# The rank-one updates of a feed-forward layer: summed into the weights ahead of the matmuls, or kept as matmuls of their own

## The chip, the cores and the metric

The kernel runs on one core of one Trainium2 chip. The metric is the device time of one launch in microseconds; of several runs the median is given. Engines are named as in the profile: PE (TensorE, matmuls), DVE (VectorE), ACT (ScalarE), POOL (GpSimd) and SP (SyncE, which issues all transfers here).

## What is computed

Two layers on 16 tokens. A "token" here is one batch entry, a matrix of 256 rows and 256 columns; `ctx` has the same shape.

```python
x = x + xattn0(ctx, layernorm(x))          # latent attention, 8 heads
x = x + ffn0(layernorm(x))                 # W1: 1024x256, W2: 256x1024
x = x + xattn1(layernorm(x), ctx, ctx)     # one head, 256 wide
x = x + ffn1(layernorm(x))                 # 8 experts, gate/up/down, routed

def ffn0(x):
    lt = x[:, 1:17, :]                     # 16 rows of each token
    even, odd = lt[:, ::2, :], lt[:, 1::2, :]
    m1 = (even[:, :4, :, None] * odd[:, :4, None, :]).reshape(Bx, Hx, Dx)
    m2 = (even[:, 4:, :, None] * odd[:, 4:, None, :]).reshape(Bx, Dx, Hx)
    h = x @ W1.T + scale * einsum('bsd,bhd->bsh', x, m1) + b1
    out = gelu(h) @ W2.T + scale * einsum('bsh,boh->bso', gelu(h), m2) + b2
```

So each token has weights of its own: W1 plus `scale` times four outer products of normalised rows of the token, one for each quarter of the 1024 hidden rows, and W2 plus four more.

## The kernel before

The kernel has two halves. The first, `latent_attention`, does the first attention for one token after the other: turns b = 0 to 15, of which 1 to 14 are a loop. The second, `ffn_attention_experts`, does the rest. Its turn t holds two things side by side: the chain of token t (feed-forward layer, second attention, routing weights) and the eight experts of token t-1. Turn 1 stands by itself, because it also splits the weights of experts 2 to 7; turns 2 to 14 are a loop, turn 15 is the last with a chain and turn 16 has experts only. The chain of token 0, which has no turn of experts to stand in, is put beside the last turn of the first half (b = 15).

All products are of float32 values split into a high and a low half in the type fp32r: a "high" copy on ACT, the difference "low" on DVE, and three matmuls for each product (high by high, high by low, low by high; lines 1818 to 1820).

The order of the work of each engine is written out by hand: each engine has its own function `turn`, which lists its instructions in the order in which its queue runs them, and semaphores say what each waits for. Between two experts stands one link of the chain: an expert has its `gate` and `up` products (24 matmuls), then ACT's silu, DVE's `hidden` (gate by up, line 1464), ACT's high copy and DVE's `hidden_low` (line 1468), then its `down` product (12 matmuls) and DVE's `weigh` (line 1481), which adds the weighted result to the token's sum `acc`. The banks of `gate` and `up` are single: `up` of the next expert waits for `hidden` of the one before. The end of a turn on PE is `gate` and `up` of expert 7, `down` 6, `transposed(t, "C")`, `z_fill(t + 1)`, `down` 7, the routing product, then `gate` and `up` of expert 0 of token t.

The chain's links are, in order: A, the transposed and normalised token (`transposed`, line 1829); H, four products into the hidden layer (`h_fill`); the gelus; Y, two products out of it (`y_fill`); the second residual; B (normalised and transposed again); V, Q, S, T, O, the parts of the second attention; C, the third normalised and transposed matrix; and R, the routing. In each of A, B and C the mean and variance are taken on DVE, the inverse deviation on POOL (`rstd_of`, lines 1031 and 1033) and the normalised matrix on DVE (`norm_apply`, line 1420).

The rank-one updates are done with matmuls. `odd_rows` (POOL) spreads the odd rows; `z_fill` multiplies them into the token (four matmuls, line 1836); `z_high` and `z_low` scale and split that; `h_fill` adds a matmul of 256 columns (line 1846) to each of its eight groups. For W2, the odd rows lie as 16 extra columns between the pieces of W2 (`W2ROW` = 272 columns), so that `y_fill` gives their products as well; `g_high` and `g_low` split these, `g_fill` transposes them (line 1858), `gt_copy` copies them and `y_update` adds them into Y (line 1864). The even rows are split by `even_high` and `even_low`, and SP brings them into place with 24 small transfers for each token, `updates_of`, into `b_up`; `h_fill` waits for these (`up_in`). W1 and W2 are loaded and split once, at the start.

Other lines in the rows below: L326 is the first half's scaling of the attention weights (`normalise_probs`, POOL), L333 its bias sum; L1044 is `bias_x2` on POOL; L1458 is `context_low`, the low half of the context on DVE; L1493 is `copy_low`, which takes the low half of a transposed matrix out of PSUM.

Of the kernel before, what the change touches and what calls it, by code (L numbers as in the profile page):

```python
# [12 lines left out]
P = 128  # L13
B = 16
# [56 lines left out]
class Beside:  # L71


    early: Callable
    beside: Callable
# [43 lines left out]
def latent_attention(nc, ctx, mem, x, ctx_in, x1, g_media, b_media, g_lat, b_lat, Wq, bq, Wkv, bkv, Wo, bo):  # L119
# [112 lines left out]
    def sections_of(eng, body):  # L232

        body(sections["first"], 0, False, True)
        with eng.Fori(1, B - 1) as b:
            body(Order(loop_names, loop_first - F, sections["first"], F, b), b, True, True)
        body(last, B - 1, True, False)

# [17 lines left out]
    def sync(sp, other):  # L256
# [24 lines left out]
        def turn(order, b, prev, nxt):  # L281
# [13 lines left out]
            if not prev:  # L295
                other.early(0)
        sections_of(sp, turn)
# [5 lines left out]
    def gpsimd(pool, other):  # L303
# [38 lines left out]
        def turn(order, b, prev, nxt):  # L342
            for h in range(H):
# [12 lines left out]
                if not prev:  # L356
                    other.early(h)
        sections_of(pool, turn)

    def scalar(act, other):  # L360
# [60 lines left out]
        def turn(order, b, prev, nxt):  # L421
            i = 0
            for h in range(H):
# [18 lines left out]
                if not prev:  # L442
                    other.early(h)
                i += n
# [5 lines left out]
    def vector(dve, other):  # L450
# [115 lines left out]
        def turn(order, b, prev, nxt):  # L566
            i = 0
            for h in range(H):
# [34 lines left out]
                if not prev:  # L603
                    other.early(h)
                i += n
# [145 lines left out]
def ffn_attention_experts(nc, ctx, mem, first, x1, ctxT, out, W1T, b1, W2T, b2, scale, Wq, bq, Wk, bk, WvT, bv, Wg, Wu,  # L751
# [21 lines left out]
    BANK = {("H", 0): 0, ("H", 1): 1, ("H", 2): 2, ("H", 3): 3, "Y0": 0, "Y1": 1, "G": 2, "V": 2, "B": 0,  # L773
            "Q": 1, "S": 3, "T": 0, "A": 2, "O": 1, "C": 3, "Z": 2, "R": 0}
# [6 lines left out]
    def put(region, name, shape, dt=F32, raw=False, odd=None):  # L781
# [4 lines left out]
    up1, up2 = put("low", "up1", [P, NL, D], F32R, odd=1), put("low", "up2", [P, D], F32R, odd=1)  # L786
    w2h, (w2_raw, w2l) = put("low", "w2h", [P, W2ROW * HC + 16], F32R, odd=1), put(
        "low", "w2l", [P, W2ROW * HC + 16], F32R, raw=True, odd=1)
    od = put("low", "od", [P, DC, P], F32R, odd=1)
    zm_part, zm = put("low", "zm_part", [P, S], F32R), put("low", "zm", [P, S], F32R, odd=0)  # L790
    gr = put("low", "gr", [P, ST, P], F32R)
    ROWS = 32
    ev1 = put("low", "ev1", [ROWS, 2, D], F32R)
    ev2 = put("low", "ev2", [ROWS, 2, NL, A4], F32R)
# [4 lines left out]
    factors = put("low", "factors", [P, 4])  # L799
    lscale, lmask, tinv, thalf = (factors[:, n:n + 1] for n in range(4))  # L800
# [31 lines left out]
    gt = put("values0", "gt", [P, ST, P], F32R, odd=1)  # L832
# [18 lines left out]
    OWN = {("H", 0): ps_c, ("H", 1): ps_x, ("H", 2): ps_c, ("H", 3): ps_x, "Y0": ps_c, "Y1": ps_x, "A": ps_c, "Z": ps_c,  # L851
# [1373 lines left out]
```

## Time and profile before

| | us |
|---|---|
| median of 3 runs | 1987.82 |
| lowest and highest | 1985.39, 1988.81 |
| the profiled execution | 1991.09 |
| its span in the trace | 1989.3 |
| mean granted TensorE clock | 0.995 of 2.4 GHz |

The profile is of one execution of its own. Its span runs from the first instruction to the last; the execution's time has 1.8 us more around it. Turn b of the first half is read between two of its residual sums, a turn of the second half as the stretch after which the pattern of instructions repeats. In the trace names that start with `a_` belong to the first half and those with `b_` to the second. Starts and durations are in us; a matmul's duration overlaps the next one's, so that what a matmul costs is read from the start of one to the start of the next.

### The profile page before, as it was taken

The page shows a single profiled execution, that of the slowest core. Times are in us where ns is not written, and L with a number is a line of the kernel's source. Part 1 is how long each engine was busy: PE and PEld are TensorE (multiplying, and loading weights), DVE is VectorE, ACT ScalarE, POOL GpSimd, SP SyncE. Part 2 cuts the span into 40 slices and gives each one's busy share as a digit, 9 for nine tenths or more (in the row PEclk, how much of TensorE's full clock was granted, in tenths as well). Part 3 has the DMA queues.
Part 4 walks back from the last instruction along what each step waited for, and adds up shares of the span by engine and source line. Part 5 has one row for each costly group of instructions (what it writes and reads, how often), then busy time and mean ns, then how long its engine had stood idle before and what let it go on. Part 6 is the DMA issues. An engine that isn't in the chain of part 4 may idle for free.

```text
span 1989.3 us, 41475 instructions
## 1 busy us (share of the span) xinstructions
PE 1927.2 (97%) x14078; PEld 1803.2 (91%) x14078; DVE 1367.9 (69%) x3408; ACT 1115.5 (56%) x2334; POOL 407.1 (20%) x650
## 2 busy tenths in 40 slices
PE   7999999999999999999987899999999999999998
PEld 6788888888888888888886899999999999999998
DVE  7877776776777776776746566766666666766665
ACT  5655565555655565555655655554555555544553
POOL 2222222222222222222213511111111101111100
PEclk9999999999999999999999999999999999999999
DMA  4000000000000000000012200000000000000000
GB/s 162 12 22 21 11 11 21 21 21 5 16 21 21 11 11 21 21 21 6 10 34 89 67 15 15 12 17 17 11 16 16 17 12 17 12 17 12 17 7 12
DMA packets 47211, 44.51 MB, mean 22 GB/s; under 512 B 6848, under 2 KB 45376, under 8 KB 47168
## 3 DMA queue, kind: packets, MB, share of 16 engines
q1 hardware_dynamic: 47168, 43.96, 6.9%
q8 instruction: 25, 0.41, 0.1%
q14 instruction: 18, 0.15, 0.0%
HBM read 34.77 MB, written 8.39 MB: 22 GB/s over the span
## 4 chain that ended last, share of the span: by engine, by line
PE 83%; DVE 7%; ACT 5%; issue 3%; POOL 1%; SPq 1%; DMA 0%; DVEq 0%; ACTq 0%; POOLq 0%
PE ring L618 9%; PE ring L620 9%; PE ring L619 9%; PE ring L1820 7%; PE ring L1818 7%; PE ring L1819 7%; PE ring L671 4%; PE sim L1818 3%; PE sim L1819 3%; PE sim L1820 3%; PE sim L618 3%; PE sim L620 2%; PE sim L619 2%; PE ps_x L1818 2%; PE ps_x L1820 2%
## 5 line engine op out<-in xcount | busy, mean ns | idle before, releaser
L411 ACT ACTIVATE a_pr<-sim,a_nmax 128x512 f32<-128x512 f32 x256 | 174.5, 689 | 208.4 <-DVE a_nmax L537 208.3
L1818 PE MATMUL ring<-b_xch,b_weh 128*128 128x256 f32 x1024 | 289.5, 283 | 1.7 <-DVE b_act_e L1464 1.7
L1819 PE MATMUL ring<-b_xcl,b_weh 128*128 128x256 f32 x1024 | 285.7, 279 | 0.0
L1820 PE MATMUL ring<-b_xch,b_wel 128*128 128x256 f32 x1024 | 285.6, 279 | 0.0
L326 POOL TENSOR_SCALAR a_pr<-a_pr,a_rinv 128x512 f32<-128x512 f32 x256 | 183.1, 729 | 498.3 <-DVE a_rinv L547 495.4
L1818 PEld LDWEIGHTS ring<-b_xch,b_weh 128*128 128x128 f32 x1024 | 192.3, 188 | 1.9 <-DVE b_act_e L1464 1.9
L1819 PEld LDWEIGHTS ring<-b_xcl,b_weh 128*128 128x128 f32 x1024 | 193.0, 188 | 0.0
L1820 PEld LDWEIGHTS ring<-b_xch,b_wel 128*128 128x128 f32 x1024 | 192.1, 188 | 0.0
L1464 DVE TENSOR_TENSOR b_act_e<-b_act_e,ring 128x512 f32<-128x512 f32 x128 | 87.9, 687 | 116.7 <-PE ring L1820 102.4
L528 DVE TENSOR_TENSOR a_ptl<-ring,a_pth 128x512 fp32r<-128x512 f32 x256 | 163.9, 682 | 3.1 <-ACT a_pth L401 2.0
L515 DVE SCALAR_TENSOR_TENSOR a_ktl<-ring,a_bkv_s,a_kth 128x512 fp32r<-128x512 f32 x128 | 95.3, 744 | 102.1 <-ACT a_kth L391 102.1
L537 DVE TENSOR_REDUCE a_nmax<-sim 128x1 f32<-128x512 f32 x256 | 163.8, 681 | 1.6 <-PE sim L620 1.6
L1179 ACT ACTIVATE b_heh<-b_act_e 128x512 fp32r<-128x512 f32 x128 | 81.1, 633 | 132.1 <-DVE b_act_e L1464 132.0
L618 PE MATMUL ring<-a_pth,a_vh 128*128 128x256 f32 x512 | 142.8, 279 | 3.7 <-DVE a_ptl L528 3.7
L524 DVE TENSOR_TENSOR a_vl<-ring,a_vh 128x512 fp32r<-128x512 f32 x128 | 88.4, 691 | 81.7 <-ACT a_vh L399 81.5
L620 PE MATMUL ring<-a_pth,a_vl 128*128 128x256 f32 x512 | 142.6, 279 | 0.0
L619 PE MATMUL ring<-a_ptl,a_vh 128*128 128x256 f32 x512 | 142.5, 278 | 0.0
L401 ACT ACTIVATE a_pth<-ring 128x512 fp32r<-128x512 f32 x256 | 140.2, 607 | 3.6 <-PE ring L671 3.6
L399 ACT ACTIVATE a_vh<-ring 128x512 fp32r<-128x512 f32 x128 | 76.8, 600 | 109.8 <-PE ring L620 109.8
L1175 ACT ACTIVATE b_act_e<-ring 128x512 f32<-128x512 f32 x128 | 76.4, 597 | 104.3 <-PE ring L1820 103.7
L671 PE MATMUL ring<-ident,a_pr 128*128 128x128 f32 x1024 | 133.3, 272 | 1.5 <-DVE a_ktl L515 1.2
L671 PEld LDWEIGHTS ring<-ident,a_pr 128*128 128x128 f32 x1024 | 118.2, 140 | 14.8 <-DVE a_ktl L515 1.5
(378 smaller groups left out, 6246.0 us busy)
## 6 DMA issues: line engine op xcount, KB each, us to landing
a_c_in<-in_ctx_in SPq DMA_DIRECT2D x16, 256.0 KB, 2.6
a_x_in<-in_x SPq DMA_DIRECT2D x16, 256.0 KB, 2.9
a_x_res<-in_x SPq DMA_DIRECT2D x16, 256.0 KB, 2.6
x_between<-a_x_out SPq DMA_DIRECT2D x16, 256.0 KB, 2.2
b_x_s<-x_between SPq DMA_DIRECT2D x16, 256.0 KB, 2.6
b_up<-b_ev SPq DMA_DIRECT2D x256, 1.0 KB
out_x<-b_acc SPq DMA_DIRECT2D x16, 256.0 KB, 2.2
b_ct_raw<-in_ctxT SPq DMA_DIRECT2D x15, 256.0 KB, 2.6
```

What stands on the lines that cost most here:

```text
L326: nc.gpsimd.tensor_scalar(pr[:, h % 2, t, :], pr[:, h % 2, t, :], rinv[:, h % 2, t:t + 1], 1.0, ALU.mult, ALU.mult).then_inc(prob_ready, 1)
L401: nc.scalar.activation(pth[:, :, name[2] * P:(name[2] + 1) * P], bank[:].rearrange("p (k q) -> p k q", k=KT), ACT.Copy).then_inc(ring_hi, 1)
L411: nc.scalar.activation(pr[:, h % 2, t, :], sim[t][:], ACT.Exp, bias=nmax[:, h % 2, t:t + 1], accum_out=rsum[:, h % 2, t:t + 1]).then_inc(e ...
L528: nc.vector.tensor_tensor(ptl[:, :, cols], bank[:].rearrange("p (k q) -> p k q", k=KT), f32(pth[:, :, cols]), ALU.subtract).then_inc(ring_ ...
L537: nc.vector.tensor_reduce(nmax[:, h % 2, t:t + 1], sim[t][:], AX.X, ALU.max, negate=True)\
L618: nc.tensor.matmul(out, lh, rh, start=(n == 0), stop=False)
L619: nc.tensor.matmul(out, lh, rl, start=False, stop=False)
L620: last = nc.tensor.matmul(out, ll, rh, start=False, stop=(n == len(parts) - 1))
L671: last = nc.tensor.transpose(bank[:, k * P:(k + 1) * P], pr[:, h % 2, t, k * P:(k + 1) * P], ident[:])
L1818: nc.tensor.matmul(out, lh, rh, start=(n == 0), stop=False)
L1819: nc.tensor.matmul(out, lh, rl, start=False, stop=False)
L1820: last = nc.tensor.matmul(out, ll, rh, start=False, stop=(n == len(parts) - 1 and not more))
```

## The change

The rank-one updates are summed into W1 and W2 themselves, for each token, one turn ahead of its chain. All rank-one matmuls and what feeds them (`odd_rows`, `z_fill`, `z_high`, `z_low`, `g_high`, `g_low`, `g_fill`, `gt_copy`, `y_update`, `even_high`, `even_low`, `updates_of`) go, and `W2ROW` is 256.

In their place, for token n: SP loads the first 32 rows of the token (`rows_load`); DVE, POOL and DVE normalise them (`rows_stats`, `rows_rstd`, `rows_apply`); SP writes 16 of them out and reads them back, the even ones spread over all partitions (`even_b`, 1 MB of SBUF) and the odd ones transposed (`rows_spread`); POOL scales the odd ones (`odd_scaled`) and makes eight updates, four pieces of W1 and four of W2, each of two products and a sum (`update`). The pieces are split anew for each token: the high halves on ACT (`weight_high`), the low halves of W1 on POOL and those of W2 on DVE (`weight_low`). W1 and W2 are loaded again for each token (1 MB each), W1 after the last of the H products and W2 after the Y products of the token before. `h_fill` waits for all low halves of W1, `y_fill` for those of W2.

```diff
+        def update(n, w, q):
+            a, b = divmod(q, 2)
...
+            for k in range(2):
...
+                nc.gpsimd.tensor_scalar(part, row, by, 1.0, ALU.mult, ALU.mult).then_inc(update_made, 1)
+            take(w_in[w], n * 16 + 16)
+            pool.wait_ge(update_made, 2 * number + 2)
+            nc.gpsimd.tensor_tensor(piece, piece, added, ALU.add).then_inc(w_eff[w], 1)
+
+        def weight_low(n, w, q):
+            take(w_hi[w], n * 4 + q + 1)
+            raw, high, low = (w_piece(w, q, tile) for tile in W[w])
+            nc.gpsimd.tensor_tensor(low, raw, f32(high), ALU.subtract).then_inc(w_lo[w], 1)
```

POOL's turn, of which only the three `rstd_of`, `row_shifts`, the two biases and `odd_rows` stood there before:

```diff
-            def turn(t, chain, more, warm):
+            def turn(t, chain, more, more2, warm):
...
+                if more:
+                    odd_scaled(t + 1)
+                    if not warm:
+                        update(t + 1, "1", 0)
                 if chain:
                     rstd_of(t, "B")
                     row_shifts(t)
                     bias_x2(t)
...
+                    update(t + 1, "1", 1)
                     rstd_of(t + 1, "A")
+                    update(t + 1, "1", 2)
+                    update(t + 1, "1", 3)
                     bias_x1(t + 1)
+                    update(t + 1, "2", 0)
+                    if more2:
+                        rows_rstd(t + 2)
+                    update(t + 1, "2", 1)
...
                 if chain:
                     rstd_of(t, "C")
                 if more:
...
+                        update(t + 1, "2", 2)
+                    update(t + 1, "2", 3)
+                    if not warm:
+                        for q in range(4):
+                            weight_low(t + 1, "1", q)
```

The chain's links on PE move by about half a slot: V goes ahead of `down` 2 and B behind it, Q ahead of `down` 3, S between `gate` and `up` of expert 5, T behind `down` 4, O and the next token's A ahead of `down` 5, C ahead of `down` 6. ACT's and DVE's orders follow. The end of DVE's turn:

```diff
                 if chain:
                     copy_low(t, "C", xcl[:], xch[:])
+                if more2:
+                    rows_apply(t + 2)
+                weigh(i, 6)
                 if more:
-                    z_low(t + 1)
-                weigh(i, 6)
+                    weight_low(t + 1, "2", 0)
+                    weight_low(t + 1, "2", 1)
                 weigh(i, 7)
+                if more:
+                    weight_low(t + 1, "2", 2)
+                    if not warm:
+                        weight_low(t + 1, "2", 3)
                 if chain:
                     hidden(t, 0)
```

In turn 1, twelve subtractions of expert weights (experts 4 to 7) move from POOL to DVE, and on ACT the high halves of the second group of experts move behind the gelus.

The first half's turn b = 14 is taken out of its loop, and what token 0 needs ahead of its chain is put there (`ahead`): its rows, POOL's updates of W1 and ACT's high halves, and the first of W2. Turn b = 15 (`beside`) holds the rest for token 0, and the updates for token 1. In the second half, turn 14 is taken out of the loop as well, since token 15 is the last to have updates made.

## Rows read from the trace of the kernel before

**Rows 1.** The page, its first part: busy us of each engine, share, instructions.

```profile
PE 1927.2 (97%) x14078; PEld 1803.2 (91%) x14078; DVE 1367.9 (69%) x3408; ACT 1115.5 (56%) x2334; POOL 407.1 (20%) x650
```

**Rows 2.** Turn windows: us, busy PE PEld DVE ACT POOL (instructions), PEclk, DMA.

```profile
940.94:1004.87 63.93, 63.57 (x402) 56.24 (x401) 44.91 (x97) 36.44 (x82) 15.35 (x26) 1.00 0.04 13
1004.87:1093.94 89.07, 71.43 (x509) 65.90 (x507) 51.74 (x114) 49.75 (x107) 19.78 (x31) 0.96 0.21 67
1102.60:1169.20 66.60, 59.58 (x468) 58.83 (x467) 40.91 (x109) 39.38 (x75) 31.43 (x33) 0.92 0.06 18
1281.40:1337.60 56.20, 55.57 (x473) 55.20 (x472) 37.70 (x109) 30.90 (x60) 8.36 (x15) 1.00 0.05 15
```

**Rows 3.** Timeline of PE: start, us, line, operation; matmuls into H, into Y.

```profile
1283.52 0.28 PE L1846 MATMUL sim<-b_zm,b_up 128*128 128x256 f32 x1
...
1283.99 0.28 PE L1818 MATMUL sim<-b_xth,b_w1h 128*128 128x256 f32 x1
...
1291.96 0.29 PE L1818 MATMUL sim<-b_w2h,b_hh 128*128 128x272 f32 x1
...
1292.95 0.29 PE L1820 MATMUL sim<-b_w2h,b_hl 128*128 128x272 f32 x1
```

**Rows 4.** Timeline of PE: transposes of B and C, up of expert 1.

```profile
1306.61 0.28 PE L1820 MATMUL ps_c<-b_wvh,b_ctl 128*128 128x256 f32 x1
1307.42 0.52 PE L1829 MATMUL sim<-ident,b_ln 128*128 128x128 f32 x3 [0.54 <-DVE b_ln L1420]
...
1328.23 0.28 PE L1820 MATMUL ring<-b_weh,b_hel 128*128 128x256 f32 x1
1328.61 0.66 PE L1829 MATMUL ring<-ident,b_ln 128*128 128x128 f32 x4
...
1335.87 0.28 PE L1818 MATMUL ring<-b_xch,b_weh 128*128 128x256 f32 x1
```

**Rows 5.** Timeline of DVE at the end of the same turn.

```profile
1329.99 0.69 DVE L1493 TENSOR_TENSOR b_xcl<-ring,b_xch 128x512 fp32r<-128x512 f32 x1 [0.70 <-ACT b_xch L1198]
...
1331.89 0.88 DVE L1481 SCALAR_TENSOR_TENSOR b_acc<-ps_x,b_wts,b_acc 128x256 f32<-128x256 f32 x2
1334.50 0.69 DVE L1464 TENSOR_TENSOR b_act_e<-b_act_e,ring 128x512 f32<-128x512 f32 x1 [1.73 <-PE ring L1820]
```

**Rows 6.** Forms by line: count, ns min/median/max, first and last start.

```profile
L1458 DVE TENSOR_TENSOR b_ctl<-b_ct_raw,b_cth x15: 680/685/686, 1117.1 to 1910.1; 128x512 fp32r<-128x512 f32 x15
L1458 DVE TENSOR_TENSOR b_ctl<-b_gel,b_cth x1: 1410/1410/1410, 1057.4 to 1057.4; 128x512 fp32r<-128x512 f32 x1
...
L326 POOL TENSOR_SCALAR a_pr<-a_pr,a_rinv x256: 692/699/1135, 30.2 to 1077.4; 128x512 f32<-128x512 f32 x128
...
L1044 POOL TENSOR_TENSOR b_x_s<-b_x_s,b_bv_b x16: 1286/1309/1732, 1058.2 to 1925.9; 128x512 f32<-128x512 f32 x16
...
L1031 POOL TENSOR_SCALAR b_rows<-b_mv x48: 192/194/433, 990.7 to 1943.8; 128x2 f32<-128x2 f32 x48
```

**Rows 7.** Timeline of POOL and DVE in the first half's last turn.

```profile
1047.57 1.71 POOL L333 TENSOR_TENSOR a_x_res<-a_x_res,a_bo_b 128x512 f32<-128x512 f32 x1
...
1048.07 1.76 DVE L1432 TENSOR_TENSOR b_wvl<-b_wvl_raw,b_wvh 128x512 fp32r<-128x512 f32 x1
```

**Rows 8.** Timeline of PE: the matmuls behind two long waits.

```profile
1014.71 0.55 PE L1818 MATMUL ps_c<-b_xth,b_w1h 128*128 128x256 f32 x1 [5.58 <-DMA b_up<-b_ev]
...
1115.94 0.56 PE L1818 MATMUL sim<-b_w2h,b_hh 128*128 128x272 f32 x1 [3.25 <-DVE b_hl L1488]
```

**Rows 9.** Windows behind these two waits, columns as in rows 2.

```profile
1013.00:1019.00 6.00, 4.29 (x20) 4.32 (x21) 0.00 (x0) 0.90 (x3) 0.03 (x1) 0.50 0.28 89
1115.00:1121.00 6.00, 5.06 (x22) 5.09 (x23) 3.47 (x7) 4.45 (x9) 1.54 (x3) 0.50 0.14 45
```

**Rows 10.** DMA issues: count, KB each, us from issue to landing.

```profile
b_w2l_raw<-in_W2T SPq DMA_DIRECT2D x1, 1024.0 KB, 8.1
```

More of the change, by code:

```diff
@@ L1020, in rest @@
             sp.wait_ge(out_done, 16 * B + 16)
-        return Beside(early, beside, rest)
+        return Beside(early, ahead, beside, rest)
     def gpsimd(pool):
@@ L1309, in beside @@
                 copy_high(1, "A", xth[:])
+            if (h, done) == (7, ("O", 6)):
+                for q in range(4):
+                    weight_high(1, "1", q)
             if (h, done) == (7, ("T", 7, 1)):
@@ L1323, in rest, with turn, experts @@
         def rest():
-            def turn(t, chain, more, warm):
+            def turn(t, chain, more, more2, warm):
                 i = t - 1
-                for e in warm_in(0) if warm else ():
-                    for j in range(3):
-                        expert_high(e, j)
+                def experts(slot):
+                    for e in warm_in(slot) if warm else ():
+                        for j in range(3):
+                            expert_high(e, j)
+                experts(0)
                 silu(i, 1)
@@ L1396, in turn @@
                     hidden_high(t, 0)
+                if more and warm:
+                    weight_high(t + 1, "2", 3)
+                if chain:
                     tanh_high(t)
             sections_of(act, turn)
-        return Beside(early, beside, rest)
+        return Beside(early, ahead, beside, rest)
     def vector(dve):
@@ L1724, in beside, with turn @@
                 distances(0)
+                for q in range(4):
+                    weight_low(1, "2", q)
         def rest():
-            def turn(t, chain, more, warm):
+            def turn(t, chain, more, more2, warm):
                 i = t - 1
@@ L1809, in turn, with product @@
                     distances(t)
+                if more and warm:
+                    weight_low(t + 1, "2", 3)
             sections_of(dve, turn)
-        return Beside(early, beside, rest)
+        return Beside(early, ahead, beside, rest)
     def tensor(pe):
-        def product(out, parts, left_h, left_l, right_h, right_l, more=False):
+        def product(out, parts, left_h, left_l, right_h, right_l):
             for n, part in enumerate(parts):
@@ L1819, in product @@
                 nc.tensor.matmul(out, lh, rl, start=False, stop=False)
-                last = nc.tensor.matmul(out, ll, rh, start=False, stop=(n == len(parts) - 1 and not more))
+                last = nc.tensor.matmul(out, ll, rh, start=False, stop=(n == len(parts) - 1))
             return last
@@ L1830, in transposed @@
             last.then_inc(full[name], 1)
-        def z_fill(n):
-            pe.wait_ge(od_ready, n + 1)
-            for c in range(DC):
-                for k, x in enumerate((xth, xtl)):
-                    last = nc.tensor.matmul(bank(n, "Z")[:, 0:S], od[:, c, :], x[:, c, :],
-                                            start=(c == 0 and k == 0), stop=(c == DC - 1 and k == 1))
-            last.then_inc(full["Z"], 1)
         def h_fill(t, n):
```

556 lines of the change are left out of this document (292 added, 264 removed).

## Prediction

> **What bounds the kernel now.** I read the busy times of the page first: TensorE (PE) is busy in 97% of the span and no other engine in more than 69% [rows 1]. So time is gained only by taking PE work away or by closing one of the short gaps in which PE waits. Next I read the windows, one per turn [rows 2]: a steady turn of the second half takes 56.2 us and PE is busy in 55.57 of it, while GpSimd (POOL) works 8.36 us and VectorE (DVE) 37.7. The first turn, which also splits the weights of six experts, takes 66.6 us; the last turn of the first half, with the chain of token 0 beside it, takes 89.07 with PE busy in 71.4. These two have the long gaps [rows 8] and stretches at half the clock [rows 9], and the rest is near solid. Then I read the PE timeline for the step from one matmul to the next and for the gaps at the chain's links [rows 3, 4], the end of a turn on DVE [rows 5], and what a DVE and a POOL instruction do to each other [rows 6, 7].
>
> **What leaves PE in a steady turn.** A 256-column matmul is issued every 0.1175 us (1283.52 to 1283.99 is four), a 272-column one every 0.124 (1291.96 to 1292.95 is eight) [rows 3]. Gone are eight rank-one matmuls of `h_fill`, four of `z_fill`, two transposes of `g_fill` and two matmuls of `y_update`: 16 x 0.1175 = 1.88 us (the two transposes are narrower, so this is a few hundredths too much). The 48 matmuls of `y_fill` become 256 columns wide: 48 x 0.0065 = 0.31. Moving the links by half a slot gives each longer between its parts: the wait ahead of the transposes of B (1306.61 to 1307.42, less one step, 0.69) and the one ahead of those of C (1328.23 to 1328.61, less one step, 0.26) [rows 4] should close. Sum 3.14: a turn of 53.1 if nothing new stalls.
>
> **What is added.** On POOL an update is two products of 128x256 and one sum of 128x512. A tensor_scalar takes 0.70 us at 512 columns and 0.19 at 2 [rows 6], so about 0.44 at 256; a sum takes 1.31. One update is 2.2 us, eight are 17.5; four subtractions for the low half of W1 add 5.2, the row statistics and the scaling of the odd rows about 1.5. With the 8.36 of before, less about 1.4 of copies, POOL works some 31 us of 56: it has the room, but not at any moment. ScalarE (ACT) gets eight copies (about 5 us) onto 30.9 and loses its small copies: covered. DVE gets four subtractions for W2 (0.685 each, 2.7 us) and loses 1.5 or so: covered by its 18 us of idle time, if they can be spread. SyncE (SP) loses 24 small transfers per token and gets two reloads of 1 MB; W2's took 8.1 us from issue to landing [rows 10] and now has half a turn, so I cost it at nothing; if it were late by half a turn, the first sum into W2 would stand still on POOL with all behind it. The spreading of the rows waits on SP for POOL's last sum into W2 of the turn before, and the store of a finished token stands behind it there; nothing reads that store within the turn.
>
> **The collision.** DVE and POOL hold each other up. The subtraction L1458 (two operands in SBUF) took 0.68 to 0.69 us fifteen times and 1.41 once [rows 6], the time at which POOL ran; POOL's L1044 rose from 1.31 to 1.73, L326 from 0.70 to 1.13, L1031 from 0.19 to 0.43. In the first half a DVE subtraction of 1.76 us that began under a POOL sum of 1.71 ended 0.55 after it [rows 7]. Reading from PSUM it isn't so held: L1493 takes its 0.69 us as always [rows 5]. Today POOL works so little that this hardly shows. After the change it works all the time, and DVE has nine two-SBUF subtractions of its own in a turn and four new ones.
>
> The Trainium skill (page "SBUF — State Buffer", section "SBUF: two separate sides") states the port pair that VectorE and GpSimd share as an exclusive lock which the first comer holds for its whole instruction. The 1.41 of [rows 6] is less than a subtraction behind a whole POOL sum would be, the 0.55 after the end in [rows 7] is what such a lock gives. By the page alone each of four subtractions would wait out a whole sum, and the stall worked out next would be about 4.0 us in place of 2.25.
>
> **Where the collision lies on the path.** At the end of a turn DVE does the low half of C, two weighings, and then `hidden(t, 0)`, which frees the bank that PE's `up` of expert 1 writes next. Before: the low half of C ends at 1329.99 + 0.69 = 1330.68, `hidden` starts at 1334.50 (it waits for PE) and ends at 1335.19, PE's `up` starts at 1335.87 [rows 4, 5]: 3.82 us between, 0.68 to spare. After: the transposes of C go ahead of down 6, twelve matmuls earlier (+1.41), and `z_fill` is gone (-0.47), so 4.76 us between, 5.44 with the slack. In it DVE must now do the rows (0.3), two weighings of 0.87 and four subtractions for W2: 0.3 + 1.75 + 4 x 0.685 = 4.8, which fits. But POOL does its own four subtractions for W1, 1.31 us each, at that very time (both sets are put last in the turn). At 1.41 each the four take 5.64 and the sum is 7.7: PE waits 2.25 us, where before it waited for nothing. If they don't meet it is 0; if each waits out a whole POOL sum (1.31 + 0.55 = 1.86 each, 7.4 together), 4.0. I take 2.25, by the row of the same DVE instruction.
>
> **Smaller new waits.** `y_fill` starts 0.94 us sooner after the matmuls that feed the gelus; the inverse deviations of B and C (0.19 + 0.70 us on POOL) can stand behind an update of 2.2 us each; DVE's subtractions of the hidden values, at 1.41 when they meet POOL, hold the `down` products; `s_fill` and `o_fill` have other neighbours. None of these is in the trace of before. Each lies between 0 and the 2.2 of one update; I take 0.3 to 0.6 each, 1.7 together (bounds 0 and 3).
>
> So a steady turn is 53.1 + 2.25 + 1.7 = 57.0, +0.8 (bounds -1.9 without the end stall and with half of the small ones, +3 with the longest end stall), 13 turns: +10.4.
>
> **The other turns.** In the first half's last turn PE waits 5.58 us for the small transfers into `b_up`, [rows 8] and runs at half clock (0.50, 1.2 GHz) for the 6 us behind that wait [rows 9]: both go, 5.58 + 3.0, and 2.2 of PE work, 10.8 in all. Against it stands POOL, which gets updates for tokens 0 and 1 between its normalisations, DVE held by them, and the deviation of C behind updates; I take 3 back (bounds 0 and 8): -8. In the turn before, 63.9 us and PE busy in 63.6 [rows 2], all added work is cost: seven updates and three subtractions, 19 us, onto POOL's 15.4, in front of normalisations that PE's transposes wait for, and DVE waits for the loaded rows: +4 (bounds 0 and 8). The first turn of the second half: ACT splits fewer expert weights ahead of the gelus, so the 3.25 us wait of `y_fill` [rows 8] and the half-clock stretch behind it [rows 9] (6 us, 3.0) can go, and PE work of 2.2; DVE takes twelve subtractions over (8.3 us) with POOL beside it: I take 5.4 back, -3 (bounds 0 and -7). The turn of the last chain has no updates: -2. Sum 10.4 - 8 + 4 - 3 - 2 = +1.4 on the profiled 1991.1 us (its span is 1989.3), 1992.5. The median of the runs shown lies 3.3 below the profiled one: 1989.
>
> **Rivals.** *The collision misses PE (chance 0.27).* DVE's four subtractions wait for ACT's copies, which follow POOL's sums one by one; if they fall between POOL's own subtractions, or POOL is done before, the end stall is gone and a turn is about 54.3: 13 x -1.9 = -24.7, with -8, +2, -4 and -2 for the other turns: -37, 1951. For it: DVE is idle a third of the turn. Against it: the orders put both at the end. *The stall takes the clock along (0.10), slower.* In the trace PE's waits of 3.25 and 5.58 us [rows 8] were each followed by some 6 us at 1.2 GHz [rows 9]; in the steady turn, whose gaps are under 1 us, the clock is full (1.00 of 2.4 GHz) [rows 2]. From an end stall of about that length on, each turn would lose 3.0 us on top, and win back the small waits (1.5), which a slow PE doesn't meet: 57.0 + 1.3 + 3.0 - 1.5 = 59.8, 13 x 3.6 = +47, about 2035. By the whole-instruction lock of the page above (4.0) this is what would happen; the row of 1.41 speaks against it. *POOL is the bound (0.03).* If its 31 us, stretched by DVE, came to more than the turn leaves ahead of `h_fill`, the turn would follow POOL; 45 us even with each sum at 1.73, so no: some 2010. *It is all hidden (0.02)*: PE work gone is made up by waits for the same DVE work, 1988.
>
> **How the numbers follow.** Forecast 0.58, 1989 us, its own range 1976 to 2004. The range for 8 in 10 takes in half of the faster rival and the upper bounds of the end stall without the clock: 1951 to 2014. About 0.2% (4 us) is what a measurement of this kernel can tell from no change. Of the forecast's 0.58 I put 0.14 below 1984, 0.20 within and 0.24 above 1992: faster 0.14 + 0.27 = 0.41, same 0.22, slower 0.24 + 0.13 = 0.37.
>
> **What would show it.** In the changed kernel's windows a steady turn with PE busy in 53 us and 57 long; in its PE timeline a gap of about 2 us at the first matmul of `up` of expert 1, released by DVE's `hidden`; L1458's kin, the W2 subtractions, at 1.4 us and not 0.69; no `b_up` gap and no 0.50 stretch in the 89 us turn. I am wrong if the W2 subtractions take 0.69, if they are done ahead of the low half of C, or if a gap above 3 us stands elsewhere in each turn.

## The result, and the profile of the changed kernel

| | before | after |
|---|---|---|
| median, us | 1986.76 | 2030.41 |
| lowest, highest | 1985.39, 1988.81 | 2029.02, 2031.3 |
| profiled execution, its span | 1991.09, 1989.3 | 2029.02, 2027.2 |

(The kernel before has one run more here than in the table ahead of the prediction.) The ratio is 1.0215, 95% interval 1.0199 to 1.0231: the change costs 2.1%, and the time lies above the predicted range. The page's first part of the changed kernel (after), to be held against [rows 1]:

```profile
PE 1913.3 (94%) x13822; PEld 1778.5 (88%) x13822; DVE 1492.3 (74%) x3442; ACT 1139.7 (56%) x2362; POOL 836.2 (41%) x1036
```

PE lost 256 matmuls and 14 us of busy time, yet the span grew by 37.9. POOL's work doubled, as meant, and DVE is busy 124 us longer. The windows of the four kinds of turn, with the columns of [rows 2] and in the same order (the last two turns of the first half, the first of the second, a steady one):

```profile
934.59:999.61 65.02, 62.93 (x395) 55.03 (x395) 46.92 (x102) 39.23 (x87) 41.42 (x53) 1.00 0.15 43
999.61:1084.38 84.77, 70.95 (x489) 65.72 (x487) 54.96 (x112) 51.62 (x108) 51.58 (x60) 0.94 0.34 101
1093.10:1168.30 75.20, 60.67 (x454) 59.18 (x453) 60.42 (x126) 40.59 (x77) 47.37 (x46) 0.89 0.24 69
1282.20:1341.40 59.20, 54.71 (x457) 53.45 (x455) 45.48 (x111) 32.60 (x61) 35.96 (x41) 1.00 0.23 68
```

Each stretch measured between the same two events of both traces, in the second half from the `hidden` of expert 0 at the end of one turn to that of the next (the predicted column is the prediction's own step; the window of b = 14 in [rows 2] starts 1.2 us ahead of its residual sum, so that the stretch of before is 62.7 and not 63.9):

| stretch | predicted, us | measured, us |
|---|---|---|
| first half, b = 0 to 13 | 0 | -7.6 |
| b = 14 | +4 | +2.3 |
| b = 15 | -8 | -4.3 |
| t = 1 | -3 | +8.3 |
| t = 2 to 14 (13 turns) | +10.4 | +39.4 |
| t = 15 and 16 | -2 | -0.3 |
| sum | +1.4 | +37.8 (spans: 37.9) |

Two lines carry the miss: the steady turns, 29.0 us beyond the forecast, and the first turn of the second half, 11.3 us. The steady turns' waits on PE's timeline (start, duration, and in brackets the idle time and its releaser; the wait runs from the start of the matmul before, less one step of 0.1175):

```profile
1282.21 0.28 PE L1917 MATMUL ring<-b_xch,b_wel 128*128 128x256 f32 x1
1284.23 0.38 PE L1915 MATMUL ring<-b_xch,b_weh 128*128 128x256 f32 x1 [1.74 <-DVE b_act_e L1564]
...
1296.55 0.36 PE L1915 MATMUL sim<-b_w2h,b_hh 128*128 128x256 f32 x1 [0.83 <-DVE b_hl L1588]
...
1322.04 0.33 PE L1990 MATMUL sim<-ident,b_pr 128*128 128x128 f32 x1 [0.78 <-ACT b_pr L1322]
...
1332.60 0.33 PE L1926 MATMUL ring<-ident,b_ln 128*128 128x128 f32 x1 [0.57 <-DVE b_ln L1507]
...
1335.07 0.39 PE L1915 MATMUL ps_x<-b_weh,b_heh 128*128 128x256 f32 x1 [0.40 <-DVE b_hel L1568]
```

The first is the end stall: 1284.23 - 1282.21 - 0.12 = 1.90 us at `up` of expert 1, released by DVE's `hidden`. Counted from the matmul ahead of each in the same way, the others are 0.99 at Y, 0.93 at T, 0.73 at C and 0.56 at `down` 7; with 0.32 at O the six make 5.43. 59.20 less these is 53.8, in which the matmuls just behind a wait take longer (0.33 to 0.39 us for 0.28).

DVE and POOL in the same turn, DVE first, in two fences. "x2" is two instructions with their time together:

```profile
1331.32 1.22 DVE L1507 TENSOR_SCALAR b_ln<-b_x_s,b_mv,b_rows 128x256 f32<-128x256 f32 x2
...
1333.83 1.18 DVE L1568 TENSOR_TENSOR b_hel<-b_act_e,b_heh 128x512 fp32r<-128x512 f32 x1 [0.70 <-ACT b_heh L1288]
...
1336.64 2.70 DVE L1525 TENSOR_TENSOR b_w2l<-b_w2l_raw,b_w2h 128x512 fp32r<-128x512 f32 x2
...
1340.04 2.69 DVE L1525 TENSOR_TENSOR b_w2l<-b_w2l_raw,b_w2h 128x512 fp32r<-128x512 f32 x2
```

```profile
1296.72 1.30 POOL L1120 TENSOR_TENSOR b_w1l_raw<-b_w1l_raw,b_rank_one 128x512 f32<-128x512 f32 x1 [9.69 <-DMA b_w1l_raw<-in_W1T]
...
1304.64 0.19 POOL L1064 TENSOR_SCALAR b_rows<-b_mv 128x2 f32<-128x2 f32 x1 [6.62 <-DVE b_mv L1500]
...
1330.95 1.44 POOL L1117 TENSOR_SCALAR b_rank_one<-b_even_b,b_odd 128x256 f32<-128x256 f32 x2
...
1337.05 6.82 POOL L1125 TENSOR_TENSOR b_w1l<-b_w1l_raw,b_w1h 128x512 fp32r<-128x512 f32 x4
```

The four W2 subtractions at the turn's end take 1.35 us each (2.70 / 2), beside POOL's four W1 subtractions of 1.71 each (6.82 / 4): the meeting that the prediction expected. But two other DVE operations, on the chain's path, are stretched as well: the two halves of the normalisation of C to 0.61 each, beside products of POOL, and `hidden_low` of expert 7 to 1.18. And POOL stands idle for 9.69 us in front of its first sum of the turn, waiting for the reload of W1, and for 6.62 more behind it, waiting for DVE's variance of B. In its order one update of eight stands ahead of B; the last two and the four W1 subtractions come at the end.

### The profile page after: what moved, and what is told of

It is laid out like the page before. It is cut to its first block, busy times and chain, and to the rows that moved or that the text cites. A ratio compares the mean times of both kernels' runs of the same rounds, so it can differ in the third digit from the quotient of the medians.

```text
span 2027.2 us, 41696 instructions
## 1 busy us (share of the span) xinstructions
PE 1913.3 (94%) x13822; PEld 1778.5 (88%) x13822; DVE 1492.3 (74%) x3442; ACT 1139.7 (56%) x2362; POOL 836.2 (41%) x1036
## 4 chain that ended last, share of the span: by engine, by line
PE 59%; DVE 19%; ACT 11%; issue 9%; POOL 1%; DVEq 1%; DMA 0%; ACTq 0%; POOLq 0%; SPq 0%
PE ring L632 9%; PE ring L634 9%; PE ring L633 9%; PE ring L685 4%; DVE b_acc L1581 3%; PE sim L632 3%; PE ring L1915 2%; PE ring L1917 2%; PE sim L634 2%; PE ring L1916 2%; PE sim L633 2%; PE sim L1915 2%; DVE b_act_e L1564 2%; PE sim L1917 2%; PE sim L1916 2%
## 5 line engine op out<-in xcount | busy, mean ns | idle before, releaser
L1117 POOL TENSOR_SCALAR b_rank_one<-b_even_b,b_odd 128x256 f32<-128x256 f32 x256 | 174.4, 694 | 10.5 <-POOL b_odd L1094 4.9
L1284 ACT ACTIVATE b_act_e<-ring 128x512 f32<-128x512 f32 x128 | 76.2, 595 | 163.7 <-PE ring L1917 163.2
L1568 DVE TENSOR_TENSOR b_hel<-b_act_e,b_heh 128x512 fp32r<-128x512 f32 x128 | 118.2, 923 | 60.0 <-ACT b_heh L1288 59.7
L1120 POOL TENSOR_TENSOR b_w1l_raw<-b_w1l_raw,b_rank_one 128x512 f32<-128x512 f32 x64 | 83.7, 1308 | 129.7 <-DMA b_w1l_raw<-in_W1T 125.5
```

Of the source, the lines that this page charges most:

```text
L1117: nc.gpsimd.tensor_scalar(part, row, by, 1.0, ALU.mult, ALU.mult).then_inc(update_made, 1)
```

## Experiments

A time without an interval is of one run, beside one run of the kernel before on the same chip.

**Links alone.** Does the new order of the links cost something by itself, or only the added work? No token but the first gets rows, updates, reloads or new splits; all use the weights of token 0.

```diff
         def update(n, w, q):
+            if not (isinstance(n, int) and n == 0):
+                return
...
-                    pe.wait_ge(w_lo["1"], t * 4 + 4)
+                    pe.wait_ge(w_lo["1"], 4)
```

> The changed kernel without its added work: from token 1 on no rows are loaded, no updates made, W1 and W2 neither loaded again nor split again (every token uses the weights of token 0). The new order of the links and the missing matmuls stay. If the added work makes the stalls (collision of DVE and POOL, or work that comes late), a steady turn falls from 59.15 us to 53.1 to 53.8 and the whole to about 1945. If the new order of the links makes them, gaps of about 1 us stay ahead of the Y products, the T products and the transposes of C, and a turn takes 56 or more, the whole 1985 or more.

Measured: 1953.1 us, before beside it 1985.92. A steady turn (columns as in [rows 2]), a little above the range of the first expectation and far below the second; and PE's matmul at its longest wait:

```profile
1495.60:1550.00 54.40, 53.90 (x455) 53.23 (x455) 36.82 (x103) 28.68 (x53) 6.73 (x9) 1.00 0.05 15
```

```profile
1545.79 0.36 PE L1934 MATMUL sim<-b_w2h,b_hh 128*128 128x256 f32 x1 [0.30 <-DVE b_hl L1607]
```

Three waits are left, counted as above: Y 0.46, C 0.25 and `down` 7 0.27, together 0.98. So 54.40 - 0.98 = 53.4 is the turn's PE work, 0.3 above the 53.1 of the prediction, and the new order costs 1.0 us of waits by itself. The other 4.8 (59.20 - 54.40) come with the added work. They don't come from PE, which does the same in both.

**Without products and sums.** The 24 operations of the updates become eight fills of one column; reloads, high halves and all eight subtractions stay where they are.

```diff
-                nc.gpsimd.tensor_scalar(part, row, by, 1.0, ALU.mult, ALU.mult).then_inc(update_made, 1)
...
-            nc.gpsimd.tensor_tensor(piece, piece, added, ALU.add).then_inc(w_eff[w], 1)
+            nc.gpsimd.memset(rank_one[:, q % 2, 0:1], 0.0).then_inc(w_eff[w], 1)
```

> The changed kernel without the products and sums of the updates: in the place of each update POOL writes one column. Reloads, high halves, the four W1 subtractions on POOL and the four W2 subtractions on DVE stay. If DVE is held by whatever POOL does, most of POOL's 24 us per turn are gone, only the subtractions can meet: the gaps ahead of T, C and down 6 fall from 1.05, 0.85 and 0.68 to below 0.4, and a turn to 54 to 55.5. If the gaps come from the order of the queues and the added instructions of DVE and ACT, they stay and a turn takes 58 or more.

Measured: 1994.88 us, a steady turn 57.2; neither expectation was met. The W2 subtractions are short, and the end stall is gone, since POOL now does its W1 subtractions earlier. But there they meet the normalisation of C and `hidden_low` of expert 7. The form by its line, then DVE, POOL and PE in one steady turn (line numbers are this kernel's):

```profile
L1516 DVE TENSOR_TENSOR b_w2l<-b_w2l_raw,b_w2h x60: 668/672/1784, 1090.6 to 1899.9; 128x512 fp32r<-128x512 f32 x60
```

```profile
1547.90 2.26 DVE L1498 TENSOR_SCALAR b_ln<-b_x_s,b_mv,b_rows 128x256 f32<-128x256 f32 x2
...
1551.46 1.64 DVE L1559 TENSOR_TENSOR b_hel<-b_act_e,b_heh 128x512 fp32r<-128x512 f32 x1 [0.70 <-ACT b_heh L1279]
```

```profile
1547.45 5.10 POOL L1116 TENSOR_TENSOR b_w1l<-b_w1l_raw,b_w1h 128x512 fp32r<-128x512 f32 x4
...
1550.22 0.65 PE L1917 MATMUL ring<-ident,b_ln 128*128 128x128 f32 x4 [1.62 <-DVE b_ln L1498]
```

The normalisation took 1.13 a half, `hidden_low` 1.64 and not 0.69, and PE waits for both: 1.78 at C and 1.03 at `down` 7, counted as above. Products and sums aren't needed for this: POOL's subtractions do it by themselves where they fall on the chain.

**POOL's time without its reads.** Is DVE held by POOL's reads, or by any work of POOL? Here the updates and the W1 subtractions become chains of small fills, which read nothing (36 fills for the four subtractions, 2.98 us in place of the 5.10 above). They are shorter than what they replace: POOL is busy in 19.0 us of a turn, not in 36.0.

```diff
+            for k in range(7):
+                nc.gpsimd.memset(tile[:, k * 256 // 7:(k + 1) * 256 // 7], 0.0)
             take(w_in[w], n * 16 + 16)
...
+            for k in range(11):
+                last = nc.gpsimd.memset(tile[:, 256 + k * 256 // 11:256 + (k + 1) * 256 // 11], 0.0)
+            last.then_inc(w_eff[w], 1)
```

> The changed kernel with POOL as busy as before but reading nothing in its added work: each product, sum and subtraction is replaced by small fills of about the same time in all (the weights keep no update and no low half of W1). If POOL's reading is what holds DVE, the W2 subtractions on DVE fall from 1.35 and more to 0.69, the end stall from 2.0 to below 0.6, and a turn to 53.5 to 55. If only the lateness of POOL's queue counts, or fills hold DVE as well, a turn stays at 58 to 59.2.

Measured: 2050.32 us, a steady turn 61.4: slower than the change itself, and neither expectation was met. A subtraction beside fills (DVE, then POOL), the form of the normalisation (ns min/median/max), then DVE, POOL and PE at one C, and PE's windows from the wait on:

```profile
1495.99 0.69 DVE L1568 TENSOR_TENSOR b_hel<-b_act_e,b_heh 128x512 fp32r<-128x512 f32 x1 [0.70 <-ACT b_heh L1288]
...
1495.91 0.65 POOL L1115 MEMSET b_rank_one<- 128x23 f32 x11
1496.49 0.51 POOL L1112 MEMSET b_rank_one<- 128x36 f32 x7
```

```profile
L1507 DVE TENSOR_SCALAR b_ln<-b_x_s,b_mv,b_rows x96: 394/409/4656, 989.3 to 2001.4; 128x256 f32<-128x256 f32 x96
```

```profile
1512.17 4.97 DVE L1507 TENSOR_SCALAR b_ln<-b_x_s,b_mv,b_rows 128x256 f32<-128x256 f32 x2
...
1513.70 2.98 POOL L1124 MEMSET b_w1l<- 128x56 f32 x36
...
1517.20 0.69 PE L1926 MATMUL ring<-ident,b_ln 128*128 128x128 f32 x2 [4.32 <-DVE b_ln L1507]
```

```profile
1512.60:1517.20 4.60, 0.28 (x4) 0.07 (x2) 4.60 (x3) 0.00 (x0) 4.08 (x57) 0.89 0.00 0
1517.20:1521.00 3.80, 3.80 (x18) 3.80 (x19) 2.32 (x5) 3.19 (x6) 0.00 (x0) 0.50 0.00 0
```

A subtraction of two operands in SBUF isn't held by fills: the low half of a hidden matrix takes its 0.69 with fills beside it from start to end. (The W2 subtractions are short as well, and the end stall is gone, but POOL is idle by then, so that these show nothing of fills.) But one half of the normalisation, with a single operand in SBUF and 0.41 us long, took 4.65, until the whole row of fills was through. PE then waits 4.32 us, and runs at 0.50 (1.2 GHz) behind it, every turn. So the two kinds of DVE operation are held by different work of POOL: the subtraction only by work that reads, the normalisation, which the prediction left out, by either.

**The first turn of the second half.** In it DVE's four W2 subtractions for token 1 stand ahead of what the gelus wait for (DVE, then POOL, of after):

```profile
1092.06 5.79 DVE L1525 TENSOR_TENSOR b_w2l<-b_w2l_raw,b_w2h 128x512 fp32r<-128x512 f32 x4
...
1092.59 4.71 POOL L1132 TENSOR_TENSOR b_wel<-b_wel_raw,b_weh 128x512 fp32r<-128x512 f32 x3 [8.92 <-ACT b_weh L1275]
...
1108.10 0.55 PE L1915 MATMUL sim<-b_w2h,b_hh 128*128 128x256 f32 x1 [5.92 <-DVE b_hl L1588]
```

Moving them behind the gelus on DVE was to take the wait away.

```diff
                 distances(0)
-                for q in range(4):
-                    weight_low(1, "2", q)
...
                         gelu_low(t, n)
+                    if warm:
+                        weight_low(t, "2", n)
```

> The changed kernel with the four W2 subtractions of token 1 moved on DVE from ahead of the first hidden product of the second half's first turn to behind each of its four gelus. If these (5.8 us beside POOL's subtractions of expert weights) delay the gelus and so the Y products, the gap of 6.2 us there falls below 3 and the first turn from 75.2 us to 68 to 71. If ACT's order or POOL delays the gelus, the gap stays above 5.

Measured: 2029.57 us, the turn 76.2 where it was 75.5 (counted as in the table of stretches). The same wait is now released by the moved subtractions themselves:

```profile
1110.16 0.55 PE L1915 MATMUL sim<-b_w2h,b_hh 128*128 128x256 f32 x1 [7.04 <-DVE b_w2l L1525]
```

So the expectation missed. Y needs all four, and both places lie ahead of it: the move leaves them on its path. A later experiment takes them off DVE.

**POOL held back for the normalisation.** If held normalisations are the cause, POOL should wait, after the inverse deviations of A and C, until DVE has normalised.

```diff
                     rstd_of(t + 1, "A")
+                    pool.wait_ge(ln_ready["A"], t + 2)
...
                     rstd_of(t, "C")
+                    pool.wait_ge(ln_ready["C"], t + 1)
```

> The changed kernel with two waits more on POOL: behind the inverse deviations of A and C it stands still until DVE has normalised. All work stays. If it is POOL's work that stretches the normalisation (0.73 us for two alone, 1.22 in the steady turn, 4.97 under a row of fills), both take 0.73 to 0.8 and the gap ahead of the transposes of C falls from 0.85 to about 0.4, the one ahead of T from 1.05 to 0.6; POOL's work ends later by what it waited (about 4 us), so that the end stall grows from 2.0. If DVE's normalisation is long for another reason, it stays at 1.2.

Measured: 2070.85 us, before beside it 1988.14. The normalisations are free in the steady turns (0.73 for two), so it was POOL's work that stretched them. But the gap ahead of C didn't fall, it grew, and all is much slower (the form by line, then DVE and PE at one C, and POOL's first product behind the A that follows):

```profile
L1509 DVE TENSOR_SCALAR b_ln<-b_x_s,b_mv,b_rows x96: 394/411/1347, 989.6 to 2023.5; 128x256 f32<-128x256 f32 x96
```

```profile
1281.51 0.73 DVE L1509 TENSOR_SCALAR b_ln<-b_x_s,b_mv,b_rows 128x256 f32<-128x256 f32 x2 [3.24 <-POOL b_rows L1066]
...
1282.30 1.12 PE L1928 MATMUL ring<-ident,b_ln 128*128 128x128 f32 x4 [3.76 <-DVE b_ln L1509]
...
1329.29 0.98 POOL L1117 TENSOR_SCALAR b_rank_one<-b_even_b,b_odd 128x256 f32<-128x256 f32 x2 [5.41 <-DVE b_ln L1509]
```

POOL stands 5.41 us for the normalisation of A, its updates come later, and the inverse deviation of C stands behind them: DVE waits 3.24 us for it. The turn shown, of 1280 to 1342, ran at a granted clock of 0.94, which is a part of the price. Freeing the operation by holding up POOL moves the wait into POOL's own queue.

**POOL's order, all work kept.** POOL makes one update ahead of B, idle for 9.69 and 6.62 us around its sum, and has two updates and all W1 subtractions at the end. Here it makes the first products while W1 is loading, does three W1 sums ahead of B, puts each W1 subtraction between two W2 updates, and waits for the normalised C before its last piece. ACT's high halves move forward with it, and one W2 subtraction on DVE.

```diff
+                    odd_scaled(n)
+                    products(n, "1", 0)
+                    products(n, "1", 1)
+                    added_in(n, "1", 0)
...
+                    update(n, "2", 0)
+                    weight_low(n, "1", 0)
...
+                    rstd_of(t, "C")
+                    take(ln_ready["C"], t + 1)
+                if more:
+                    update(n, "2", 3)
+                    weight_low(n, "1", 3)
```

> The changed kernel with POOL's work spread over the steady turn: both first products while W1 is on its way, three sums into W1 ahead of the deviation of B, the W1 subtractions between the sums into W2, POOL still while C is normalised; ACT's high copies and one of DVE's W2 subtractions moved to fit. Every instruction is kept. If the stall at the end comes from both subtractions being put there together, it falls from 2.0 to below 0.7 and a turn from 59.15 to 55.5 to 57, the whole to 1975 to 2000. If the collisions cost the same wherever they stand, a turn stays above 58.

With it, in a second kernel, the W2 subtractions for token 1 are done by POOL ahead of the first turn:

```diff
-                for q in range(4):
-                    weight_low(1, "1", q)
+                for w in "12":
+                    for q in range(4):
+                        weight_low(1, w, q)
```

> As the run before, and the four W2 subtractions of token 1 made by POOL ahead of the second half's first turn instead of by DVE at its start. If DVE's 5.8 us there delay the gelus, the gap of 6.2 us ahead of the Y products falls below 2.5 and the first turn from 75.2 us to 69 to 72, the whole by 3 to 6. If POOL is late with them, the gap stays above 5 and is released by them.

Measured: 2004.36 and 1995.16 us, before 1988.14 beside both. The steady turn is 57.15 and its end stall 0.32 instead of 1.9: the stall fell as the first branch said, the turn and the whole ended just above its ranges. In the second kernel the first turn of the second half is 68.9 instead of 75.5 (76.5 in the first kernel), and its wait at Y:

```profile
1104.90 0.36 PE L1970 MATMUL sim<-b_w2h,b_hh 128*128 128x256 f32 x1 [1.61 <-DVE b_hl L1642]
```

That is 9.2 us less in all, more than the 3 to 6 expected: 7.5 are this turn, and 1.8 are the last one, where a stretch at half clock is missing. So the same instructions, in another order and four of them on another engine, take 35 us less than after.

**The waits that were left** (C, `down` 7, Y, T) in three further steps, each on top of the one before. First: `down` 1 ahead of Y, the maxima ahead of the normalisation of A, that of C ahead of the weighing, the deviation of C earlier on POOL.

```diff
+                down(i, 1)
                 if chain:
...
                         y_fill(t, k)
-                down(i, 1)
```

> As the run before (POOL's work spread, token 1's W2 subtractions on POOL), and each of the gaps left in its steady turn of 57.2 us given cover: down of expert 1 ahead of the Y products instead of behind them; DVE takes the softmax maxima ahead of A's normalisation, and C's normalisation ahead of a weighing; POOL takes C's deviation ahead of a W1 subtraction. If the gaps (1.1 ahead of Y, 0.66 ahead of T, 0.42 ahead of O, 1.35 ahead of the transposes of C) are single late links, they fall to 0.3 and less, a turn to 54.3 to 55.3 and the whole to 1955 to 1975, below the kernel before. If DVE as a whole is too late because POOL holds it (6 us more of it in a turn), closing one gap opens the next and a turn stays at 56.3 or more, the whole above 1982.

Measured: 1992.15 against 1990.47, ratio 1.0008 (0.9998 to 1.0018). The turn is 56.5: Y and T are closed, but C waits 1.35 and `down` 7 1.37 (the 1.47 of the next expectation counts the step in). That is the second branch: closing the gaps opened others, where the next piece of POOL's work met the next DVE operation. Second: the deviation of C ahead of the third W2 sum, a weighing behind `hidden_low` 7, no W2 subtraction ahead of it.

```diff
-                    update(n, "2", 2)
+                    products(n, "2", 2)
...
+                    added_in(n, "2", 2)
                     weight_low(n, "1", 2)
```

> As the run before, with the two gaps of 1.47 us that were left in its steady turn taken on: POOL takes C's deviation ahead of the third sum into W2, DVE the weighing of expert 5 behind the hidden product of expert 7 and its first W2 subtraction behind the low half of C; in the second half's first turn ACT takes the tanh of the routing ahead of the last W2 copy. If these gaps stem from where single instructions stand, both fall below 0.4, a turn to 53.7 to 55 and the whole to 1955 to 1972. If POOL's hold on DVE only moves on, the same time shows at the first matmul of up of expert 1 or at down 7 and a turn stays at 56 or more, the whole above 1982.

Measured: 1980.19 against 1990.05, ratio 0.9952 (0.9935 to 0.9968), the turn 55.6, between the two branches. C is closed. One long wait is left, in ten of the eleven turns from 3 to 13 at `down` 7 (DVE, POOL, PE of one of them):

```profile
1603.34 1.83 DVE L1622 TENSOR_TENSOR b_hel<-b_act_e,b_heh 128x512 fp32r<-128x512 f32 x1
...
1603.33 1.29 POOL L1133 TENSOR_TENSOR b_w1l<-b_w1l_raw,b_w1h 128x512 fp32r<-128x512 f32 x1
...
1605.22 0.39 PE L1966 MATMUL ps_x<-b_weh,b_heh 128*128 128x256 f32 x1 [1.37 <-DVE b_hel L1622]
```

A POOL subtraction that starts 0.01 us before `hidden_low` makes that 1.83 us, 1.14 more than its 0.69, and PE waits 1.37. Third: POOL waits for `hidden_low` of expert 7 before its last W1 subtractions, and the last piece of W2 is split in the next turn, beside the gelus.

```diff
+                    pool.wait_ge(he_lo, t * E)
                     weight_low(n, "1", 2)
-                    update(n, "2", 3)
                     weight_low(n, "1", 3)
+                    update(n, "2", 3)
```

> As the run before, with the last piece of W2 split in the next turn, beside the gelus (its copy on ACT, its subtraction on DVE), and POOL still until DVE has the low half of expert 7's hidden values, before its last two W1 subtractions and its last update. In the run before, one W1 subtraction that began 0.01 us ahead of that low half made it 1.83 us instead of 0.69 and PE waited 1.65 at down 7; in other turns ACT's last W2 copy held the routing copy by 1.34. If these two are what is left, a turn falls from 55.6 to 54 to 54.6 and the whole to 1952 to 1966. If the hold moves to another of DVE's subtractions, a turn stays above 55.

Measured: 1974.15 against 1990.21, ratio 0.9927 (0.9911 to 0.9944), with a turn of 55.4 in the mean, above the range of the first branch. This beats both kernels: 0.7% less than before and 56 us less than the change as it was made. A steady turn:

```profile
1491.20:1546.50 55.30, 54.21 (x456) 53.22 (x456) 41.92 (x111) 32.65 (x61) 37.01 (x41) 1.00 0.25 72
```

POOL works 37 us, even more than in after (35.96), but DVE's busy time fell from 45.48 to 41.92 with the same 111 instructions: 3.6 us a turn of holding up are gone, and the turn is 3.9 shorter.

## Why the prediction was wrong, step by step

**What held.** The PE work of a turn, 53.1: 53.4 in the kernel with the links alone. Of the waits ahead of the transposes of B and C of [rows 4] the first closed in that kernel; the second stayed at 0.25. The end stall, predicted 2.25 at `up` of expert 1 and released by `hidden`, measured 1.90 in the same place; the W2 subtractions, predicted 1.41 by [rows 6], measured 1.35. The wait for `b_up` of [rows 8] is gone. That a copy out of PSUM isn't held is right as well, though its row doesn't show it, since POOL was idle beside L1493 of [rows 5]: in after the same low half of C takes 0.68 in each of the 14 turns in which POOL works beside it.

**The term that failed: the smaller waits of a steady turn.** Taken as 1.7 with an upper bound of 3. The measured turn is 59.18 (mean of t = 3 to 13): 53.4 of PE work, 1.9 of end stall and 3.9 for the rest. That rest is 2.2 more than forecast; the 0.3 more of PE work and the 0.35 less of end stall cancel. Over 13 turns it is some 28 of the 36 us by which the sum was short. Two reasons. Of the waits in this rest, 3.5 us, 1.0 is there without any added work (links alone): a cost of the new order that I had sized together with the collisions. The other 2.5 came with the added work, and there my list of held DVE operations was too short: I counted subtractions with two operands in SBUF, and had the normalisation at its 0.41. In after it is 0.61 a half, in no_sums 1.13, under fills up to 4.66. The waits at C and `down` 7 stand right behind a held normalisation and a held `hidden_low`. The wait at T stands behind DVE's maxima, which had the row statistics and the held normalisation of A ahead of them; it closed when the maxima went first (the first of the three later steps). Half a microsecond at Y has no held operation behind it; it is there where the end stall is and not in no_sums, where Y waits 0.43, and no run isolates it.

The Trainium skill has the missing item. Its page "VectorE: DVE Perf Modes" (section "Mode 2×_2P — use both read ports for one tensor") says that a float32 operation on a single tensor in SBUF gets its double rate by using both read ports. The Trainium skill's page "SBUF — State Buffer" (section "SBUF: two separate sides") gives such operations the same lock against any GpSimd operation, and two-operand ones only against a GpSimd operation that reads. The fills agree on both counts: 4.66 us for the normalisation, 0.69 for the subtraction. The prediction used the second page only for the price of one hold, where its list of who is held was worth more.

**POOL's order.** "It has the room, but not at any moment" was right and was not followed to its end. POOL's first sum waits 9.69 us for the reload of W1; I had costed the reloads at nothing and named only W2's. The load itself is quick (5.0 us from issue to landing), but it is issued only after the last H product. Yet that wait pushes nothing to the end by itself, for POOL is idle for 6.62 us more right behind it. What puts its work on C, `hidden_low` 7 and the end is the order, with a single update ahead of B. The other order was worth 26 us (2004.36 against 2030.41), although its first sum stands 13 us behind `hidden(t, 0)` as in after and waits for W1 as well. That run moved copies of ACT and a subtraction of DVE too, so that the share of each move isn't shown. After the 9 us of token 1's subtractions the three later steps gave another 21 (1995.16 to 1974.15).

**The first turn of the second half, -3 predicted, +8.3 measured.** I asked what the wait of 3.25 at Y would lose when ACT has less to do, and didn't walk DVE's new order: four subtractions for W2, 5.79 us, stand ahead of the `hidden` that ACT's next instructions wait for. The wait grew to 5.92. With these four on POOL it is 1.61 and the turn 6.6 us shorter; moving them on DVE didn't help. The forecast comes near the new order without the added work: with the links alone the turn is 63.5, against 67.2 before and 75.5 in after.

**b = 15, -8 predicted, -4.3 measured.** The long wait and its slow clock went as said. But the clock falls further on, so that the sign "no 0.50 stretch" failed (windows of after, columns as in [rows 2]):

```profile
1064.00:1072.00 8.00, 6.01 (x37) 5.83 (x38) 3.64 (x8) 5.16 (x10) 7.66 (x10) 0.79 0.12 31
1072.00:1080.00 8.00, 5.63 (x34) 5.27 (x32) 4.55 (x10) 2.70 (x6) 7.66 (x9) 0.79 0.61 198
```

PE waits 2.56, 1.67 and 2.01 us close together here, and the granted clock is 0.79 in the mean of 16 us (two stretches of 3.4 us at 0.50), where before it was 1.00 from 1021 on. POOL is full here (7.66 of 8), but the clock falls without that too: with the links alone, where nothing is made for token 1, the waits in these places are 2.26, 1.67 and 1.88, the turn has 10.2 us at 0.50, as in after, and takes 81.9 us. So the added work for token 1 costs 2.9 us of the 84.8; why the clock falls, where similar waits (2.26, 1.19 and 1.94) left it at 1.00 before, stays open.

**A gain that I didn't see.** The first half is 7.6 us shorter, 6.3 of it in its first turn. There the split of W1, which the change moves behind the loop, stood on DVE ahead of the first low halves of k (before, DVE and PE):

```profile
68.20 1.23 DVE L1427 TENSOR_TENSOR b_w1l<-b_w1l_raw,b_w1h 128x1024 fp32r<-128x1024 f32 x1 [1.66 <-ACT b_w1h L1145]
...
72.93 0.50 PE L618 MATMUL sim<-a_kth,a_qth 128*128 128x512 f32 x1 [2.63 <-DVE a_ktl L515]
```

In after the same `a_ktl` starts at 68.26, not at 72.12. Behind that wait of 2.63 the clock was at 0.50 for 3.4 us before and stays at 1.00 in after, which is some 1.7 of the 6.3. That the split is the whole of the rest is argued from the two traces, not shown by a run. Turn 15, without updates, is 2.1 us shorter, as forecast. Turn 16 is 1.8 longer: its wait at `up`, 1.71 before, is 2.06, and 3.4 us at 0.50 follow it, where before the clock stayed at 1.00.

**The rivals.** The slower rival's number, 2035, came near by luck: its mechanism is not what made the miss. In 12 of the 13 steady turns of after the clock is 1.00 behind the wait at the end (1.65 to 1.74 us idle), and in one it falls behind the same wait, for 3.4 us:

```profile
1341.40:1401.10 59.70, 55.91 (x457) 54.84 (x455) 46.26 (x111) 32.60 (x61) 36.24 (x41) 0.97 0.22 66
```

Behind longer waits it shows: under the fills, 4.32 us of waiting were followed by 0.50, and with POOL held back (a wait of 3.76) the turn of 1280 to 1342 ran at 0.94. The faster rival, that the collision misses PE, is near what the last kernel (spread_next) is: 55.4 a turn, where the rival said 54.3. It takes an order made for it.

## What to carry to other kernels

When work goes to GpSimd, write down which VectorE operation runs beside each piece, and which of those another engine waits for: the hold costs little where nobody waits behind it, and its whole delay on a link of the chain. Scalings of a single float32 operand in SBUF belong on that list as much as two-operand subtractions; reading from PSUM didn't. Look at where an engine with time to spare stands idle, and whether its order lets it work there: the same work in another order, with four subtractions on another engine, was worth 56 us of 2030.

## What the runs showed of the hardware that was not expected

A row of POOL fills without a pause lets no waiting normalisation in between: the one of 0.41 us took 4.66 under such a row. Beside a row of POOL subtractions it got its turn (1.13 a half in no_sums), as two-operand subtractions do: 1.35 each beside 1.71 each, at the end of the turn in after. And those run freely beside fills, at 0.69. A wait of 1.65 to 1.74 us at the same place in each of 13 turns left the granted clock at 1.00 twelve times and was followed by 3.4 us at 0.50 once.
